# Layer 1's norm, half copies and value copies on ACT, early projections, late stores

## The chip, the core and the metric

The kernel runs on one core of a Trainium2 chip. The core has five engines with a queue of their own each: TensorE (PE, with its weight loads as PEld), VectorE (DVE), ScalarE (ACT), GpSimd (POOL) and SyncE (SP, which here issues DMAs). An engine works through its queue in order; a semaphore that it waits for holds up everything behind. The metric is the device time of the whole program in microseconds (us), less is better.

## The reference

The input is x, 32 x 256 x 128 in float32. Two transformer layers follow each other, each an attention part and a feed-forward part with a layer norm after each residual.

```python
# layer 0
qkv = x @ w_qkv + b_qkv          # 16 heads of 8; q and v also get a low-rank term
out = softmax(q k^T * 8**-0.5) v @ w_proj + b_proj
x = layernorm(x + out)
x = layernorm(x + experts(x))    # top-2 of 8 experts; one with over 1.25*tokens/8 tokens is dropped
# layer 1
q, k = rope(x @ w_q), rope(x @ w_k); v = x @ w_v      # causal, no bias
x = layernorm(x + softmax(masked q k^T * 8**-0.5) v @ w_proj)
x = layernorm(x + 0.1 * spline(x)) * gamma + beta
```

## The kernel before

Four stages run one after the other: attention of layer 0 (`attention`, "attn0"), the routing of the experts (`moe`), attention of layer 1 ("attn1") and the spline part with its norms. In `moe` only the routing is computed as a rule; a flag on the chip says whether any expert keeps its tokens, and here the branch with the experts isn't taken.

**An attention stage** is a pipeline over the 32 sequences. In a step st each engine works on several sequences at once, told apart by a lag: `st.has(2)` and `st.seq(2)` speak of the sequence that entered two steps ago. Lag 0: q and k, split in three bfloat16 parts by GpSimd, stored to `attn_scratch` in HBM and, at lag 1, loaded again by SyncE in six DMAs of 192 KB as stacks `q_st`, `k_st`. Lag 2: row scores (L665; in layer 1 with a mask, L661), whose maxima VectorE takes from three PSUM banks (L475), splits (L486, L488) and TensorE transposes (L594); ACT copies them (L451 for the first half of the heads, L426 for the second), SyncE places them in `q_st`. Values are projected (L631) and copied by VectorE (L499 in layer 0, L502 in layer 1). Lag 3: column scores (L687, mask L683), Exp on ACT (L419), value sums (L704). Lag 4: output copied (L441), transposed (L620), divided by VectorE (L509, L513), transposed (L638, copy L446), projected (L644), added to x (L528), statistics (L532, L538), norm.

The norm of layer 0 is GpSimd's (L338 to L367). In layer 1 GpSimd computes rstd (L338, L340) and VectorE the two tiles (L543, function `layer_norm`).

**The order in a step** is written by hand in the table `AT`: all engines count n from 0 to 15, one head's or unit's scores each, and an entry such as `act_mT1=1` says after which n the piece stands in that engine's queue. `pe_pv` does so for the value sums as (lag, unit). `pipeline` writes the first DEPTH steps out, then a loop of three steps, then the rest.

**Layer 1's q and k** are projected ahead for all sequences (`front`, TensorE L716). ACT copies those of sequences 0 to 2 straight to `qk` and, with the partition halves exchanged, to `q_half` (L388, L390); the others go to `probs` (L396) and in groups of four to HBM (`attn_qk_scratch`, L403, 1 MB each). Twenty are done before the first step, twelve within step 2, between its first row scores; in step 3 ACT waits for all stores before its first Exp. From sequence 3 on SyncE loads q and k (L237, 256 KB) and the two exchanged halves (L239, 128 KB each) one step ahead, and GpSimd rotates them: times sin (L311), times cos (L312), sum (L315). GpSimd then makes the parts (L320, L325, L329, L332), and in front of L325 it waits for the split of the first half's maxima, to leave VectorE alone.

## Time and profile before

| | us |
|---|---|
| median of 3 runs | 1414.62 |
| lowest, highest | 1412.3, 1417.19 |
| the profiled execution, its own time | 1410.58 |
| its span, first to last instruction | 1408.9 |
| busy in the span: PE, DVE, ACT, POOL | 1096.9, 1035.9, 778.3, 626.9 |
| mean granted TensorE clock | 0.885 |

Layer 0's attention lies at some 20 to 548 us of the span, the routing at 548 to 583, layer 1's attention at 583 to 1184, the spline part behind it. A busy time is the sum of an engine's instructions; idle time is told with what released the engine ("<-"). The granted clock is the share of 2.4 GHz that TensorE was given; 0.5 is 1.2 GHz.

### The profile page before, as it was taken

Reading aid. Unit: us, or ns where it says so; the run is one execution under the profiler, and the core shown is the slowest. Engines: PE = TensorE matmul, PEld = TensorE weight load, DVE = VectorE, ACT = ScalarE, POOL = GpSimd, SP = SyncE. Lnnn points to the kernel's source line nnn. Section 1 sums busy time; section 2 is a strip of 40 time slices with the busy share of each in tenths; the row PEclk is TensorE's granted clock in tenths of the full one; section 3 lists DMA queues with packets and bytes.
Section 4 is the critical chain, followed back from the end, with each engine's and each line's share of the span. In section 5 each row is a group of like instructions: output and inputs, shape, how many; then the busy total and the mean of one; then the engine's idle time right before and its main releaser. Section 6 shows DMA issues by size and latency. Waiting matters only on the chain. (4 is left out here: it accounts for less than half of the span.)

```text
span 1408.9 us, 36010 instructions
## 1 busy us (share of the span) xinstructions
PE 1096.9 (78%) x11349; PEld 803.1 (57%) x11349; DVE 1035.9 (74%) x2676; ACT 778.3 (55%) x1727; POOL 626.9 (44%) x845
## 2 busy tenths in 40 slices
PE   4799999999999996478888888888888897701330
PEld 3466666666666654356776777777777784401220
DVE  3688888888888871435877777777777772598886
ACT  2376776776776774335555555545555464500675
POOL 3245555555555532343544444444444414100666
PEclk9799999999999998798999999989999898855555
DMA  7545445445445410196656666655666521100012
GB/s 194 140 117 129 122 115 129 119 117 129 119 118 130 120 46 2 40 290 165 144 134 141 140 142 142 140 125 132 142 139 140 133 52 53 67 0 1 21 40 60
DMA packets 124967, 155.98 MB, mean 111 GB/s; under 512 B 13506, under 2 KB 100962, under 8 KB 115682
## 3 DMA queue, kind: packets, MB, share of 16 engines
q1 hardware_dynamic: 118114, 147.25, 42.8%
q10 hardware_dynamic: 6784, 7.86, 1.7%
q8 instruction: 36, 0.59, 0.2%
q14 instruction: 33, 0.27, 0.1%
HBM read 96.04 MB, written 45.35 MB: 100 GB/s over the span
## 5 line engine op out<-in xcount | busy, mean ns | idle before, releaser
L475 DVE TENSOR_REDUCE attn_negmax<-attn_row_ps 128x2 f32<-128x512 f32 (+1 forms) x1024 | 599.6, 618 | 202.5 <-PE attn_row_ps L665 190.6
L419 ACT ACTIVATE attn_probs<-attn_col_ps 128x512 f32<-128x512 f32 (+1 forms) x1024 | 532.9, 542 | 239.9 <-PE attn_col_ps L687 227.6
L687 PE MATMUL attn_col_ps<-q_st,k_st 74*128 74x256 bf16 (+1 forms) x2048 | 375.3, 265 | 16.4 <-ACT attn_probs L419 14.3
L665 PE MATMUL attn_row_ps<-k_st,q_st 72*128 72x256 bf16 (+1 forms) x2048 | 376.5, 266 | 8.8 <-DMA k_st<-attn_scratch 7.8
L687 PEld LDWEIGHTS attn_col_ps<-q_st,k_st 74*128 74x128 bf16 x2048 | 184.4, 100 | 99.5 <-ACT attn_probs L419 48.0
L704 PE MATMUL attn_out_ps<-attn_probs,v_sb 128*32 128x256 f32 (+1 forms) x4096 | 228.8, 356 | 0.7 <-ACT attn_probs L419 0.7
L665 PEld LDWEIGHTS attn_row_ps<-k_st,q_st 72*128 72x128 bf16 x2048 | 204.7, 100 | 36.6 <-issue 8.8
L661 PE MATMUL attn_row_ps<-mask_qk,ident_h 128*128 128x256 bf16 x512 | 147.3, 288 | 67.3 <-DVE attn_negmax L475 59.8
L704 PEld LDWEIGHTS attn_out_ps<-attn_probs,v_sb 128*32 128x32 f32 x4096 | 122.3, 110 | 71.1 <-issue 20.2
L325 POOL TENSOR_TENSOR attn_rest<-attn_qk,attn_parts 128x512 f32<-128x512 f32 x64 | 74.1, 1158 | 188.1 <-DVE attn_mparts L488 187.8
L683 PE MATMUL attn_col_ps<-mask_kq,ident_h 128*128 128x256 bf16 x512 | 147.3, 288 | 9.2 <-ACT attn_probs L419 5.1
L338 POOL TENSOR_SCALAR attn_var<-attn_mv 128x2 f32<-128x2 f32 x64 | 14.3, 223 | 292.8 <-DVE attn_mv L538 292.8
L543 DVE TENSOR_SCALAR x_mid<-attn_y_sb,attn_mv,attn_rstd 128x128 f32 (+1 forms) x64 | 70.7, 1145 | 39.8 <-POOL attn_rstd L340 39.8
L661 PEld LDWEIGHTS attn_row_ps<-mask_qk,ident_h 128*128 128x128 bf16 x512 | 51.5, 101 | 84.1 <-DVE attn_negmax L475 66.6
L1664 POOL TENSOR_TENSOR ffn_rstd<-ffn_var,minus_half 128x8 f32<-128x8 f32 x19 | 31.8, 1676 | 105.4 <-DVE ffn_var L1686 103.9
L332 POOL TENSOR_TENSOR attn_parts<-attn_rest,attn_parts 128x512 bf16<-128x512 f32 x64 | 74.0, 1156 | 5.4
L320 POOL TENSOR_SCALAR attn_parts<-attn_qk 128x512 bf16<-128x512 f32 x64 | 39.5, 617 | 68.2 <-ACT attn_qk L434 40.1
L683 PEld LDWEIGHTS attn_col_ps<-mask_kq,ident_h 128*128 128x128 bf16 x512 | 51.7, 101 | 27.7 <-issue 9.3
L1594 PE MATMUL ffn_o_ps<-ident_h,ffn_onehot 128*128 128x128 bf16 x64 | 10.1, 313 | 70.2 <-PEq L1345 70.2
L1605 PE MATMUL ffn_r_ps<-table_hm,ffn_ohT 128*128 128x193 bf16 x64 | 21.0, 361 | 55.9 <-ACT ffn_ohT L1617 55.9
L311 POOL TENSOR_TENSOR attn_q_half<-attn_q_half,sin 128x512 f32<-128x512 f32 x32 | 40.5, 1267 | 41.3 <-ACT attn_q_half L390 38.2
L446 ACT COPY attn_onT_sb<-attn_fin_ps 128x256 f32<-128x256 f32 x64 | 23.7, 370 | 60.0 <-PE attn_fin_ps L638 60.0
(232 smaller groups left out, 1668.8 us busy)
## 6 DMA issues: line engine op xcount, KB each, us to landing
q_st<-attn_scratch SPq DMA_DIRECT2D x192, 192.0 KB
k_st<-attn_scratch SPq DMA_DIRECT2D x192, 192.0 KB
attn_scratch<-attn_parts SPq DMA_DIRECT2D x64, 384.0 KB, 2.8
attn_scratch<-attn_parts SPq DMA_DIRECT2D x64, 128.0 KB, 2.8
attn_qk<-attn_qk_scratch SPq DMA_DIRECT2D x29, 256.0 KB, 7.6
attn_q_half<-attn_qk_scratch SPq DMA_DIRECT2D x58, 128.0 KB, 7.7
attn_qk_scratch<-attn_probs ACTq DMA_DIRECT2D x7, 1024.0 KB, 9.3
attn_xT<-x_mid SPq DMA_DIRECT2D x32, 128.0 KB, 2.4
```

What stands on the lines that cost most here:

```text
L311: nc.gpsimd.tensor_tensor(q_half_, q_half_, sin, ALU.mult).then_inc(sin_done, 1)
L320: nc.gpsimd.tensor_scalar(parts[:, :, 0, :], qk_, 1.0, 0.0, ALU.mult, ALU.add)\
L325: nc.gpsimd.tensor_tensor(rest[:, :, :], qk_, parts[:, :, 0, :], ALU.subtract)\
L332: nc.gpsimd.tensor_tensor(parts[:, :, 2, :], rest[:, :, :], parts[:, :, 1, :], ALU.subtract)\
L419: nc.scalar.activation(probs_of(st, 3, u)[:, j, 0:W], col_ps[:, n % 2, 0:W], ACT.Exp, scale=scale).then_inc(probs_kept, 1)
L475: nc.vector.tensor_reduce(negmax[:, t, 2 * p:2 * p + 2], row_ps[:, row_bank(st, u), 0:2 * keys].rearrange("p (a k) -> p a k", a=2), AX_X, ...
L543: nc.vector.tensor_scalar(x_all[:, bass.ds(st.seq(4, TB, t), 1), :].rearrange("p t c -> p (t c)"), y_sb[:, t, :], mv[:, t, 0:1], rstd[:, t ...
L661: nc.tensor.matmul(seen[:, :, keys - P:keys], ident_h[:, :], mask_qk[:, :, :], start=True, stop=False, skip_group_check=True)
L665: last = nc.tensor.matmul(bank[:, a * keys:(a + 1) * keys], q_st[0:KROWS, sl, h, t * P:(t + 1) * P], k_st[0:KROWS, sl, h, 0:keys], start=n ...
L683: nc.tensor.matmul(seen[:, :, 0:P], ident_h[:, :], mask_kq[:, :, :], start=True, stop=False, skip_group_check=True)
L687: last = nc.tensor.matmul(bank[:, t * N:(t + 1) * N - first], k_st[0:rows, sl, h, t * P:(t + 1) * P], q_st[0:rows, sl, h, first:N], start= ...
L704: last = nc.tensor.matmul(out_ps[32 * j:32 * j + 32, g * N + first:(g + 1) * N], v_sb[:, st.slot(lag), t, 32 * h:32 * h + 32], probs_of(st ...
```

## The change

- Layer 1's norm goes from VectorE to ACT (`ln_on="act"`): GpSimd also computes shift = -rstd * mean, and ACT writes rstd * y + shift. It runs one step later (`ln_lag=5`), so DEPTH is 6. Layer 0's stays on GpSimd at lag 4.
- Layer 1's value copies go from VectorE to ACT, after n=8.
- q_half is no longer loaded. ACT copies the halves from `qk` after n=15 (`HALF_ON="act"`), once its load has landed; GpSimd waits for these copies.
- 15 projections of layer 1 (0 to 14) move into `moe`, behind the last logits, and three groups are stored from there; the Exp of the second half of the routing (`weigh(1)`) stands after the fourth. 17 stand before layer 1's first step, none within step 2. The last four stores are issued in step 2, once the first stacks have landed, and each Exp group of step 3 waits for its own.
- `give` says at which GpSimd operations it waits for VectorE's split: in layer 0 before the third part (`lo`) instead of `rest`, in layer 1 before both.
- Several places in `AT` move by one to four.
- `probs`, `qk`, `q_half` are allocated once for both layers; the experts' buffers lie in `probs`. In the branch not taken here, the projections are done again.

```diff
-AT = {"attn0": dict(act_mT1=1, act_qk=(2, 4), act_oT=(4, 4), act_onT=8, act_mT0=11,
-                    dve_o=7, dve_split0=8, dve_split1=15, dve_v=5, dve_y=13, dve_var=15,
-                    pe_mT1=2, pe_qk=1, pe_oT=6, pe_v=5, pe_onT=8, pe_mT0=10, pe_y=12,
...
+AT = {"attn0": dict(act_mT1=2, act_qk=(3, 4), act_oT=(4, 5), act_onT=8, act_mT0=10, act_v=None, dve_o=6,
...
+                    pe_pv={8: [(3, 0), (3, 1)], 14: [(3, 2)], 4: [(4, 3)]}, give={"ln": [1], "lo": [0]}, ln_lag=4,
+                    ln_on="pool"),
...
+                    give={"lo": [0], "rest": [0]}, ln_lag=5, ln_on="act")}
+HALF_ON = "act"
-DEPTH = 5
+DEPTH = 6
-FRONT_EARLY = 20
+FRONT_MOE = 15
+STORED_MOE, STORED_LATE = 3, 4
...
-                for to, of_row in ((0, P // 2), (P // 2, 0)):
+                for to, of_row in ((0, P // 2), (P // 2, 0)) if HALF_ON == "dma" else ():
                     sp.dma_start(q_half[to:to + P // 2, sl, :, :].rearrange("p s n -> p (s n)"),
...
+                if ln_on == "act":
+                    pool.wait_ge(rstd_kept, st.seq(LN, c=1))
+                    nc.gpsimd.tensor_tensor(shift[:, :], rstd[:, :], mv[:, :, 0], ALU.mult).then_inc(product_kept, 1)
+                    pool.wait_ge(product_kept, st.seq(LN, c=1))
+                    apart(pool, mem)
+                    nc.gpsimd.tensor_scalar(shift[:, :], shift[:, :], -1.0, 0.0, ALU.mult, ALU.add)\
+                        .then_inc(shift_kept, 1)
...
+                        if HALF_ON == "dma":
+                            pool.wait_ge(qk_loaded[st.slot(0)], st.turn(0, 16 * QK_LOADS, -16 * QK_LOADS))
+                        else:
+                            pool.wait_ge(half_kept, st.seq(SLOTS, 2, 2))
...
+                    if fronted and not st.loop and st.off == 2 and n < PROBS:
+                        if n == 0:
+
+                            act.wait_ge(q_stacked[0], 16 * STACKS)
+                            act.wait_ge(k_stacked[0], 16 * STACKS)
+                        store_front(STORED_LATE + n)
...
+                    if fronted and HALF_ON == "act" and n == at["act_half"] and st.has(-1) and \
+                            (st.loop or st.off >= SLOTS - 1):
+                        sl = st.slot(-1)
+                        act.wait_ge(qk_loaded[sl], st.turn(-1, 16 * QK_LOADS, -16 * QK_LOADS))
+                        for to, of_row in ((0, P // 2), (P // 2, 0)):
+                            nc.scalar.copy(q_half[to:to + P // 2, sl, :, :].rearrange("p s n -> p (s n)"),
+                                           qk[of_row:of_row + P // 2, sl, :, :].rearrange("p s n -> p (s n)"))\
+                                .then_inc(half_kept, 1)
+                    if n == at["act_v"] and st.has(2):
+                        act.wait_ge(v_ready, st.seq(2, c=1))
...
+                    if ln_on == "act" and n == at["act_ln"] and st.has(LN):
+                        act.wait_ge(shift_kept, st.seq(LN, c=1))
...
+                pe.wait_ge(xT_kept, 2 * GROUPS)
+                for b in range(FRONT_MOE):
+                    if b >= 4:
+                        pe.wait_ge(front_kept, kept_by(b - 4))
+                    project(b, front_ready)
                 for half in range(2):
                     pe.wait_ge(routed, COUNTED * (half + 1))
...
-                weigh(1)
+                for b in range(FRONT_MOE):
+                    if b == WEIGH_BEFORE:
+                        weigh(1)
+                    act.wait_ge(front_ready, b + 1)
+                    keep_qk(b, front_kept)
```

Layer 1, ACT's queue from its second copy of the output (L441) to the end of a step; before, L451 and L446 are the copies of the maxima and of the transposed output.

```order
L441 COPY attn_oT_sb<-attn_out_ps 128x256
L419 ACTIVATE attn_probs<-attn_col_ps 128x384 x4
L451 COPY attn_mT_sb<-attn_in_ps 16x256
L419 ACTIVATE attn_probs<-attn_col_ps 128x384 x4
L446 COPY attn_onT_sb<-attn_fin_ps 128x256
L419 ACTIVATE attn_probs<-attn_col_ps 128x384 x2
```

The same stretch of the change, where L450 is the Exp, L504 and L477 the two copies named above.

```order
L472 COPY attn_oT_sb<-attn_out_ps 128x256
L450 ACTIVATE probs<-attn_col_ps 128x384 x4
L493 COPY v_sb<-attn_in_ps 128x8x2x8 x2
L498 ACTIVATE x_mid<-attn_y_sb,attn_shift,attn_rstd 128x128 x2
L450 ACTIVATE probs<-attn_col_ps 128x384
L504 COPY attn_mT_sb<-attn_in_ps 16x256
L450 ACTIVATE probs<-attn_col_ps 128x384 x4
L477 COPY attn_onT_sb<-attn_fin_ps 128x256
L450 ACTIVATE probs<-attn_col_ps 128x384 x2
L483 COPY q_half<-qk 64x512 x2
```

Four copies and two norm instructions have come in: values and norm behind the ninth Exp, the halves at the step's end.

The routing stage, TensorE's queue from the last logits to the counts, before:

```order
L883 MATMUL moe_t_ps<-ident,x_mid 128x128 x8
L895 MATMUL moe_g_ps<-x_all,moe_gate_T 32x256 x4
L905 MATMUL moe_l_ps<-ident,moe_gates_sb 128x128 x2
L905 MATMUL moe_l_ps<-ident,moe_gates_sb 128x128 x4
L912 MATMUL moe_g_ps<-moe_counts,moe_ones 128x8 x2
```

and in the change:

```order
L964 MATMUL moe_t_ps<-ident,x_mid 128x128 x8
L976 MATMUL moe_g_ps<-x_all,moe_gate_T 32x256 x4
L986 MATMUL moe_l_ps<-ident,moe_gates_sb 128x128 x2
L986 MATMUL moe_l_ps<-ident,moe_gates_sb 128x128 x4
L891 MATMUL moe_t_ps<-x_all,wqk 128x256 x30
L998 MATMUL moe_g_ps<-moe_counts,moe_ones 128x8 x2
```

Thirty projection matmuls, two a sequence, stand in front of the counts.

Layer 0, ACT's queue in the first third of a step: L426 copies the second half's maxima, L434 the projected q and k, L441 the output. Before:

```order
L419 ACTIVATE attn_probs<-attn_col_ps 128x512 x2
L426 COPY attn_mT_sb<-attn_fin_ps 16x256
L419 ACTIVATE attn_probs<-attn_col_ps 128x512
L434 ACTIVATE attn_qk<-attn_in_ps,bqk 128x256
L419 ACTIVATE attn_probs<-attn_col_ps 128x512 x2
L434 ACTIVATE attn_qk<-attn_in_ps,bqk 128x256
L441 COPY attn_oT_sb<-attn_out_ps 128x256 x2
```

In the change:

```order
L457 COPY attn_mT_sb<-attn_fin_ps 16x256
L450 ACTIVATE probs<-attn_col_ps 128x512
L465 ACTIVATE qk<-attn_in_ps,bqk 128x256
L450 ACTIVATE probs<-attn_col_ps 128x512
L465 ACTIVATE qk<-attn_in_ps,bqk 128x256
L472 COPY attn_oT_sb<-attn_out_ps 128x256
L450 ACTIVATE probs<-attn_col_ps 128x512
L472 COPY attn_oT_sb<-attn_out_ps 128x256
```

Three Exps stand before the copy of the maxima (L457) now instead of two, one Exp between it and the first of q and k as before, and an Exp has come between the two copies of the output.

## Rows read from the trace of the kernel before

**Rows 1.** Stretches: busy us (x count), PE, PEld, DVE, ACT, POOL; clock; DMA; GB/s.

```profile
100.00:493.00 393.00, 381.47 (x3896) 252.82 (x3895) 334.31 (x780) 280.36 (x598) 214.95 (x364) 1.00 0.50 122
614.00:632.50 18.50, 17.26 (x98) 13.35 (x99) 9.19 (x20) 6.75 (x12) 6.03 (x6) 0.90 0.89 268
699.80:1133.60 433.80, 377.16 (x4452) 311.26 (x4450) 335.46 (x800) 223.38 (x526) 205.11 (x225) 0.93 0.59 136
842.30:860.10 17.80, 15.58 (x178) 12.78 (x178) 13.36 (x33) 8.94 (x21) 8.20 (x9) 0.90 0.56 134
860.10:876.30 16.20, 13.93 (x178) 11.62 (x178) 13.30 (x34) 8.86 (x21) 8.22 (x10) 1.00 0.62 145
1136.70:1150.90 14.20, 13.86 (x180) 11.72 (x178) 11.29 (x33) 8.99 (x21) 0.93 (x2) 1.00 0.38 87
```

**Rows 2.** Groups of 699.8 to 1133.6 us, ACT: xcount, busy us, mean ns, idle before.

```profile
L446 ACT COPY attn_onT_sb<-attn_fin_ps 128x256 f32<-128x256 f32 x25 | 9.2, 367 | 0.0
```

**Rows 3.** Waits of 699.8 to 1133.6 us: us in total, times, longest.

```profile
PE attn_row_ps L661 <- DVE attn_negmax L475: 56.6, 25, 2.3
```

**Rows 4.** DVE and PE in time: start, us, engine, line; [idle before, releaser].

```profile
849.11 1.51 PE L704 MATMUL attn_out_ps<-attn_probs,v_sb 128*32 128x256 f32 x32
...
857.69 2.51 DVE L543 TENSOR_SCALAR x_mid<-attn_y_sb,attn_mv,attn_rstd 128x128 f32 x2 [1.25 <-POOL attn_rstd L340]
...
860.58 0.28 PE L661 MATMUL attn_row_ps<-mask_qk,ident_h 128*128 128x256 bf16 x1 [2.25 <-DVE attn_negmax L475]
...
1150.43 0.60 DVE L543 TENSOR_SCALAR x_mid<-attn_y_sb,attn_mv,attn_rstd 128x128 f32<-128x128 f32 x2 [1.25 <-POOL attn_rstd L340]
...
1151.42 0.28 PE L661 MATMUL attn_row_ps<-mask_qk,ident_h 128*128 128x256 bf16 x1 [0.35 <-DVE attn_negmax L475]
```

**Rows 5.** Line L543 (min/median/max ns), and GpSimd in order of time.

```profile
L543 DVE TENSOR_SCALAR x_mid<-attn_y_sb,attn_mv,attn_rstd x64: 341/1290/1308, 669.5 to 1182.7; 128x128 f32 x48, 128x128 f32<-128x128 f32 x16
...
857.62 1.27 POOL L311 TENSOR_TENSOR attn_q_half<-attn_q_half,sin 128x512 f32<-128x512 f32 x1
```

**Rows 6.** ACT at a step's end, in time; then lines L390 and L1624.

```profile
856.69 0.36 ACT L426 COPY attn_mT_sb<-attn_fin_ps 16x256 bf16<-16x256 bf16 x1 [0.57 <-PE attn_fin_ps L594]
...
L390 ACT COPY attn_q_half<-attn_col_ps x6: 577/580/582, 585.8 to 590.1; 64x512 f32<-64x512 f32 x6
...
L1624 ACT ACTIVATE ffn_z<-ffn_y,ffn_shift,ffn_rstd x64: 477/478/494, 1304.2 to 1394.3; 128x128 f32<-128x128 f32 x64
```

**Rows 7.** SyncE's issues in order of time; then landings of L237's loads.

```profile
857.08 0.70 SPq L249 DMA_DIRECT2D q_st<-attn_mT_sb  x1
...
860.60 0.38 SPq L237 DMA_DIRECT2D attn_qk<-attn_qk_scratch  x1
...
DMA to landing us min/median/max: 7.0/7.6/8.2
```

**Rows 8.** The change-over in order of time: ACT, TensorE, GpSimd, SyncE.

```profile
571.92 0.42 ACT L947 ACTIVATE moe_probs<-moe_left 128x256 f32<-128x256 f32 x1 [5.86 <-DVE moe_left L973]
...
583.15 3.75 PE L716 MATMUL attn_col_ps<-x_all,wqk 128*128 128x256 f32 x8 [2.74 <-PEq L1013]
...
587.11 1.27 POOL L311 TENSOR_TENSOR attn_q_half<-attn_q_half,sin 128x512 f32<-128x512 f32 x1 [38.23 <-ACT attn_q_half L390]
...
595.28 0.40 SPq L277 DMA_DIRECT2D attn_scratch<-attn_parts  x1
...
601.84 0.38 SPq L260 DMA_DIRECT2D q_st<-attn_scratch  x1
...
614.13 0.37 PE L661 MATMUL attn_row_ps<-mask_qk,ident_h 128*128 128x256 bf16 x1 [7.51 <-DMA k_st<-attn_scratch]
...
637.28 0.87 ACT L419 ACTIVATE attn_probs<-attn_col_ps 128x384 f32<-128x384 f32 x2 [6.99 <-DMA attn_qk_scratch<-attn_probs]
```

**Rows 9.** Waits of 100 to 480 us, TensorE's and ACT's.

```profile
PE attn_col_ps L687 <- ACT attn_probs L419: 10.4, 25, 0.5
...
ACT attn_mT_sb L426 <- PE attn_fin_ps L594: 29.0, 25, 1.2
```

More of the change, by code:

```diff
@@ L287, in step @@
             def step(st):
+                if LN == 5 and st.has(LN):
+                    finish_norm(st)
                 if st.has(4) and not fronted:
@@ L372, in _ @@
+                if LN == 4 and st.has(LN):
+                    finish_norm(st)
             pipeline(pool, step)
@@ L457, in _ @@
             if fronted:
-                for b in range(FRONT_EARLY):
+                for b in range(FRONT_MOE, B):
                     front(b)
@@ L562, in step @@
                         variance(st)
-                    if name not in LN_ON_POOL and n == at["dve_ln"] and st.has(4):
+                    if ln_on == "dve" and n == at["dve_ln"] and st.has(LN):
                         layer_norm(st)
@@ L721, in step @@
                 for n in range(H):
-                    if fronted and not st.loop and st.off == 2 and FRONT_EARLY + n < B:
-                        front(FRONT_EARLY + n)
                     if st.has(3):
@@ L754, in _ @@
             if fronted:
-                for b in range(FRONT_EARLY):
+                for b in range(FRONT_MOE, B):
                     front(b)
@@ L824, in moe, with front_bank, project, keep_qk @@
         e_h = sb("e_h", [P, MT, C])
-        e_hT = sb("e_hT", [P, MT * P])
-        e_y = sb("e_y", [P, MT, C])
-        e_acc = sb("e_acc", [P, MT, C])
         t_ps = ctx.enter_context(nc.psum_tensor("moe_t_ps", [P, 2, 2, 512], F32))
         g_ps = ctx.enter_context(nc.psum_tensor("moe_g_ps", [P, 2, 512], F32))
+        front_ready, front_kept, front_stored = (mem[k] for k in ("front_ready", "front_kept", "front_stored"))
+        redo_ready, redo_kept, redo_stored = sem("redo_ready"), sem("redo_kept"), [sem(f"redo_stored{n}") for n in range(STORED_MOE)]
+        qk, q_half, qk_dram = mem["qk"], mem["q_half"], mem["qk_dram"]
+        def front_bank(b):
+            return t_ps[:, b // 2 % 2, b % 2, :]
+        def project(b, ready):
+            for s in range(2):
+                last = nc.tensor.matmul(front_bank(b)[:, s * N:(s + 1) * N], mem["wqk1"][:, s, :], xT_all[:, b, :],
+                                        start=True, stop=True)
+            last.then_inc(ready, 1)
+        def keep_qk(b, kept):
+            of = front_bank(b)
+            if b < SLOTS:
+                nc.scalar.copy(qk[:, b, :, :].rearrange("p s n -> p (s n)"), of).then_inc(kept, 1)
+                for to, of_row in ((0, P // 2), (P // 2, 0)):
+                    nc.scalar.copy(q_half[to:to + P // 2, b, :, :].rearrange("p s n -> p (s n)"),
+                                   of[of_row:of_row + P // 2, :]).then_inc(kept, 1)
+            else:
+                nc.scalar.copy(stage[:, b - SLOTS, :], of).then_inc(kept, 1)
+        def store(act, n, stored):
+            first, to = STORED[n]
+            act.dma_start(qk_dram[first:to].rearrange("b p n -> p b n"), stage[:, first - SLOTS:to - SLOTS, :])\
+                .then_inc(stored, 16)
         l_ps = ctx.enter_context(nc.psum_tensor("moe_l_ps", [P, 2, 512], F32))
@@ L1128, in _ @@
                         nc.scalar.copy(xT_flat[:, n * 512:(n + 1) * 512], t_ps[:, 0, n % 2, :]).then_inc(again_kept, 1)
+                    for n in range(STORED_MOE):
+                        act.wait_ge(front_stored[n], 16)
+                    for b in range(FRONT_MOE):
+                        act.wait_ge(redo_ready, b + 1)
+                        keep_qk(b, redo_kept)
+                        n = group_ending(b)
+                        if n is not None:
+                            act.wait_ge(redo_kept, kept_by(b))
+                            store(act, n, redo_stored[n])
+                    for n in range(STORED_MOE):
+                        act.wait_ge(redo_stored[n], 16)
                 with act.Else():
```

209 lines of the change are left out of this document (119 added, 90 removed).

## The prediction

> **What bounds the kernel now.** I read the busy times by stretch first, then the waits of the long stretches, then the order of work in one step. In layer 0 TensorE is busy 381.5 of 393 us [rows 1] and its only wait of note is one of 0.4 us for ACT, once a step: 25 of them lie in 380 us [rows 9], so a step takes 15.2 us. In layer 1 no engine is full: TensorE 377 of 433.8 us, VectorE 335, ACT 223, GpSimd 205, and the granted clock is 0.93 [rows 1]. There 25 steps [rows 2] take 17.35 us each. The waits say why: in each of the 25 steps TensorE stands still 2.26 us (56.6 / 25) until VectorE frees a bank of row scores [rows 3]. The timeline shows what VectorE does meanwhile: it waits 1.25 us for the rstd from GpSimd, and its two norm instructions then take 2.51 us instead of the 0.60 us that they take at the end of the layer; there TensorE's stall is 0.35 us instead of 2.25 [rows 4].
>
> Two neighbouring steps show what the stall costs beyond itself. One takes 16.2 us at a granted clock of 1.00, the next 17.8 us at 0.90, with the same 178 matmuls [rows 1]: after some of the stalls TensorE runs at its lower level (1.2 GHz) for a while. A step of 14.2 us at 1.00, the one with the 0.35 us stall, exists at the layer's end [rows 1, 4]. So 17.35 is some 13.9 us of matmuls (TensorE's busy time at full clock), 2.3 us of stall and some 1.1 us of lower clock.
>
> **Layer 1, the norm.** It leaves VectorE: two instructions of 1.25 us, their wait of 1.25 us and, with them, two value copies. Why one takes 1.29 us as a rule and 0.34 at best: the median is the duration of the GpSimd multiplication that starts beside it (1.27 us) [rows 5]. VectorE waits for GpSimd here, and a norm on ACT ends that whatever ACT's price. The Trainium skill, page "SBUF — State Buffer", section "Who interferes with whom", says the same of the cause: such an instruction and a GpSimd one need one port pair, the later of the two blocks, and ACT is outside it. The page "ScalarE: Activation LUTs", section "Rules for kernel authors", speaks against the change: multiply, add and the like belong on VectorE. By it the norm should stay there, and by the rows without GpSimd beside it that would be cheaper (0.34 against 0.48 us); in this stretch the trace has 1.25 us, so the row decides.
>
> What it adds to ACT in a step: two norm instructions of 0.48 us, as the same operation takes in the last stage; two half copies of 64x512 that replace two DMAs, 0.58 us each from PSUM (from SBUF I allow 0.65); two value copies, each under the 0.36 us of a copy of 256 columns [rows 6]. That is 0.96 + 1.2 + 0.6 = 2.8 us on an engine that is busy 223 / 25 = 8.9 us a step, so 11.7 of 14.6: it doesn't bind by its sum, only by its place. GpSimd gets two small instructions more, at a place where it later waits for VectorE anyway; they cost nothing. VectorE keeps less than 335.5 - 50 x 1.25 = 273 us, 10.9 us a step.
>
> Place by place. Values and norm stand after the ninth Exp, and TensorE now has its value sums for two units there, 1.5 us [rows 4]. ACT's block is 1.5 us as well and TensorE may run two Exps ahead: hidden, but the transposed maxima behind it wait for the value copies; I allow 0.1 us. The half copies stand after the last Exp of a step. In front of TensorE there are the output projection and two heads of scores before it needs the next Exp, and ACT has some 0.6 us of slack there (its idle time before its next copy is of that size [rows 6]), so of the 1.2 us some 0.6 reach TensorE. The step becomes 13.9 + 0.6 + 0.1 = **14.6 us**, with no stall over 0.6 us; layer 0 has stalls of 0.4 us in each step and a clock of 1.00 [rows 1, 9], so I expect 1.00 here too. Ends: 14.0 (both hidden) and 16 (below). Gain: 25 x (17.35 - 14.6) = **68.8 us**.
>
> **The new wait.** ACT now waits for the load of q and k with its whole queue, the next step's Exps, behind it, and TensorE behind these. SyncE issues that load 3.5 us after the second half's maxima are handed over (857.08 to 860.60), and it lands 7.0 to 8.2 us later [rows 7]. From the hand-over to the landing: 3.5 + 7.6 = 11.1; then halves 1.2, Exp 0.5, scores and transposed maxima 1.2, their copy 0.4: a loop of 14.4 us, just under my 14.6. Two of nine DMAs, 256 of about 1,660 KB of a step's loads in that burst, are gone, which should take up to 1 us off the landing. So the loop doesn't bind, but has little room.
>
> **The change-over.** Removed: 20 projections before layer 1 and 12 between its first row scores. Now 15 run while VectorE routes, 17 follow, and half of their stores wait. The price first: four batches of copies (3 x 3 x 0.58 + 0.58 = 5.8 us, and 1 us until the first is there) stand before the Exp that VectorE's routing waits for, and ACT had only 5.9 us of idle time before it [rows 8]; the count matmul queues behind the last projection. I take +1.5 us; +7 if TensorE's clock stays low there. Then GpSimd starts its rotation at once, not 4.0 us into layer 1 (583.1 to 587.11). Its parts are stored from 595.28, the loads of the stacks start at 601.84, and the first row scores at 614.13 [rows 8]: 6.5 and 12.3 us beside stores of 1 MB. With at most two such stores around, I take 4 and 8.3: row scores at 583.1 + 1.5 + 8.0 + 0.3 + 4 + 8.3 = 605, 9 us earlier. The first step then has no projections in it (18.5 us before at 268 GB/s [rows 1]), but the late stores, 3.25 MB, start just then and share the queues with the next stack's 1.15 MB: 4.4 MB / 268 = 16 us for all, about 9 for the stacks if shared evenly, issued some 2 us in. Then half copies of 1.2 us. First Exp of the layer at 605 + 14 + 1 = 620 instead of 637.3, where ACT waited 7.0 us for the last store [rows 8]. Gain **17 us**; ends 8 (TensorE slow in the routing stage) and 24.
>
> **Layer 0.** ACT's copy of the maxima moves from behind the second Exp, where it waits 1.2 us a step for TensorE, to behind the third; with it goes the reason of TensorE's wait of 0.4 us [rows 9]. The other shifts by one place have slack of an Exp or more. The norm on GpSimd starts a little sooner; GpSimd's `rest` no longer gives way to VectorE, which may stretch a small cast. Of 30 x 0.4 = 12 I take **8 us**; ends 12 and -3. The end of layer 1 costs 0.5 us more (two GpSimd instructions and ACT's slower pair).
>
> **Sum.** 68.8 + 17 + 8 - 0.5 = 93.3 us off the profiled execution's 1410.6: 1317.3. The median of the runs is 4.0 us above that execution, so **1321 us**. Own range: steady step 14.2 to 15.1 (10 us down, 12 up), change-over 7 and 9, layer 0 4 and 11, hardly all on one side: 1303 to 1340.
>
> **Rivals.**
> A, 22%: the loop over the load binds. The landing is 8.6 us or more, since ACT's delay moves SyncE's bursts together, and steps take 15.4 to 16. At 15.7: 1321 + 25 x 1.1 = 1349. For it: 14.4 against 14.6. Against: fewer bytes, and landings within 7.0 to 8.2.
> B, 8%: ACT's bursts (2.8 us in two places) stall TensorE over 1 us, and its clock drops in every second step as now (1.6 us for 16.2 against 17.8). 13.9 + 1.2 + 0.8 + 0.1 = 16.0: 1321 + 35 = 1356. Against: the stalls of layer 0.
> C, 3%, slower: the same loop as in A, but with the load landing over 12 us after its issue. A step is then 6.8 + landing; the whole is slower than before once the step passes 17.35 + 24.5 / 25 = 18.3, a landing of 11.5. With 13 us: 19.8, so 25 x (19.8 - 14.6) = +130, 1451. For it: ACT waited 7.0 us for 1 MB stores. Against: no qk landing over 8.2 in 28.
> D, 2%: the change doesn't bring what it says: TensorE's stall only changes its releaser from VectorE to ACT at its old length; steps 17.3, and the change-over gains nothing either: within 4 us of 1415.
> The forecast has 65%.
>
> **How the numbers follow.** The likeliest case gives 1321. From 1303 up to 1352 takes in its range and most of A and part of B; some 1 in 6 is left out. About 0.3% (4 us) is what a measurement of this kernel can tell from no change: faster 0.95, same 0.02, slower 0.03.
>
> **What would show it.** Right: VectorE's releases of TensorE in layer 1 under 0.5 us a step, clock 1.00 there, steps of 14.4 to 14.8; ACT's idle time before the half copies near zero. A: ACT waits for the DMA of q and k in every step. B: clock 0.93 and TensorE waiting for ACT over 1 us. Change-over: first row scores near 605, first Exp near 620; wrong if the projections in the routing stage take 1.9 us each. Layer 0: TensorE's wait for ACT gone, steps of 14.8. Most open are the landing of the one load that ACT now waits for and the changed order in layer 0.

## The result, and the profile after

The changed kernel takes 1304.03 us (median of 4 runs, 1302.14 to 1305.4); the kernel before 1415.44 us beside it (4 runs, 1412.3 to 1417.19). The ratio is 0.9214, with a 95% interval of 0.9192 to 0.9236: 111 us less, where 94 were forecast. The profiled execution has a span of 1300.4 us against 1408.9, so 108.5 us to be explained.

Where they went, by marks that both traces have (the last reduction of layer 0 and the first Exp of each step of layer 1):

| stretch | before, us | after, us | difference | forecast |
|---|---|---|---|---|
| start to the last reduction of layer 0 | 521.8 | 497.5 | -24.3 | -8 |
| from there to layer 1's first Exp | 115.5 | 102.1 | -13.4 | -17 |
| its steps 1 to 4 | 62.5 | 60.5 | -2.0 | - |
| 25 steady steps of layer 1 | 433.8 | 365.6 | -68.2 | -68.8 |
| the rest | 275.3 | 274.7 | -0.6 | +0.5 |

The stretches of after in the columns of [rows 1] come first (span of the stretch; busy us and count of TensorE, its weight loads, VectorE, ACT and GpSimd; granted clock; DMA share; GB/s). The first is the start of layer 1, the second its 25 steady steps, the third 380 us of layer 0.

```profile
582.00:600.00 18.00, 9.02 (x61) 6.41 (x59) 8.69 (x20) 2.47 (x6) 4.30 (x5) 0.69 0.97 303
660.10:1025.70 365.60, 352.38 (x4445) 288.02 (x4445) 266.63 (x699) 281.88 (x674) 215.20 (x275) 1.00 0.59 144
100.00:480.00 380.00, 379.97 (x3992) 263.17 (x3992) 335.07 (x797) 278.01 (x612) 218.89 (x371) 1.00 0.53 130
```

A steady step of layer 1 takes 365.6 / 25 = 14.62 us at a granted clock of 1.00, where it took 17.35 at 0.93 [rows 1]. TensorE's wait in the same stretch, answering to [rows 3] (us in total, times, longest):

```profile
PE attn_col_ps L736 <- ACT probs L450: 12.5, 24, 1.5
```

The half copies (min/median/max ns) and what ACT waited for ahead of them (us, times):

```profile
L483 ACT COPY q_half<-qk x49: 616/616/617, 659.5 to 1011.2; 64x512 f32<-64x512 f32 x49
...
  DMA qk<-qk_scratch: 1.6, 2
```

TensorE waits no more for VectorE; what is left is 0.5 us a step for ACT. ACT waited for the load twice in 25 steps, 1.6 us together. The place of that last stall, in time (start, us, engine, line; in brackets the idle time before and its releaser):

```profile
864.70 1.26 ACT L483 COPY q_half<-qk 64x512 f32<-64x512 f32 x2
...
865.99 0.49 ACT L450 ACTIVATE probs<-attn_col_ps 128x384 f32<-128x384 f32 x1
866.53 0.10 PEld L736 LDWEIGHTS attn_col_ps<-mask_kq,ident_h 128*128 128x128 bf16 x1 [0.77 <-ACT probs L450]
866.53 0.28 PE L736 MATMUL attn_col_ps<-mask_kq,ident_h 128*128 128x256 bf16 x1 [0.49 <-ACT probs L450]
```

The half copies stand in front of the next step's first Exp, and TensorE waits for that Exp, as the sum had it (0.6 us there, 0.49 here). The change-over, answering to [rows 8]:

```profile
548.44 0.42 DVE L1069 TENSOR_REDUCE moe_total<-moe_probs 128x32 f32<-128x256 f32 x1 [1.21 <-ACT moe_probs L1033]
...
559.60 1.27 POOL L379 TENSOR_TENSOR q_half<-q_half,sin 128x512 f32<-128x512 f32 x1 [35.75 <-POOLq L1107]
...
567.77 0.40 SPq L289 DMA_DIRECT2D attn_scratch<-attn_parts  x1
...
571.72 0.38 SPq L272 DMA_DIRECT2D q_st<-attn_scratch  x1
...
581.50 3.60 ACTq L431 DMA_DIRECT2D qk_scratch<-probs  x4
581.57 0.37 PE L714 MATMUL attn_row_ps<-mask_qk,ident_h 128*128 128x256 bf16 x1 [4.71 <-DMA k_st<-attn_scratch]
...
590.36 0.75 SPq L280 DMA_DIRECT2D q_st<-attn_mT_sb  x1
...
597.91 1.26 ACT L483 COPY q_half<-qk 64x512 f32<-64x512 f32 x2 [8.94 <-DMA qk<-qk_scratch]
...
598.84 0.37 PE L736 MATMUL attn_col_ps<-mask_kq,ident_h 128*128 128x256 bf16 x1 [7.99 <-DMA q_st<-attn_mT_sb]
```

GpSimd starts its rotation with the layer, the stacks' loads start 4.0 us later than the store of the parts, and row scores start 9.85 us after that. Then TensorE waits 8 us for an 8 KB load (L280), issued beside 3.25 MB of late stores and right behind the next stacks' loads (1.15 MB), at 303 GB/s and a DMA share of 0.97.

Layer 0's surprise is in the waits of TensorE's weight loads. Those of 100 to 480 us, first of the kernel before, with its stretch:

```profile
PEld attn_col_ps L687 <- ACT attn_probs L419: 35.5, 76, 0.8
...
PEld attn_out_ps L704 <- ACT attn_probs L419: 5.3, 25, 0.2
```

```profile
100.00:480.00 380.00, 368.87 (x3760) 244.62 (x3759) 323.49 (x757) 271.24 (x577) 206.97 (x352) 1.00 0.50 123
```

and then of after:

```profile
PEld attn_col_ps L740 <- ACT probs L450: 21.9, 54, 0.4
...
PEld attn_out_ps L757 <- ACT probs L450: 0.2, 1, 0.2
```

Before, weight loads waited for ACT (35.5 + 5.3) / 25.1 steps = 1.63 us a step, while TensorE's own row showed 0.4 [rows 9]. After, it is 22.1 / 26.6 = 0.83, and TensorE has no idle row at all. Steps fell from 15.14 to 14.31 us. Half of the 0.83 us between the steps was hidden in busy time: 368.87 us / 3760 matmuls = 98.1 ns each before, 379.97 / 3992 = 95.2 ns after, at the same clock, which is 0.44 us over the 150 matmuls of a step.

### The profile page after: what moved, and what is told of

Its sections match the earlier page's. It is cut to its first block and busy times, and to the rows that moved or that the text cites. A ratio compares the mean times of both kernels' runs of the same rounds, so it can differ in the third digit from the quotient of the medians.

```text
span 1300.4 us, 36147 instructions
## 1 busy us (share of the span) xinstructions
PE 1060.4 (82%) x11349; PEld 785.9 (60%) x11349; DVE 948.1 (73%) x2548; ACT 841.0 (65%) x1913; POOL 640.9 (49%) x909
## 5 line engine op out<-in xcount | busy, mean ns | idle before, releaser
L450 ACT ACTIVATE probs<-attn_col_ps 128x512 f32<-128x512 f32 (+1 forms) x1024 | 531.0, 542 | 129.3 <-PE attn_col_ps L740 121.8
L718 PE MATMUL attn_row_ps<-k_st,q_st 72*128 72x256 bf16 (+1 forms) x2048 | 368.0, 261 | 8.3 <-DMA k_st<-attn_scratch 7.4
L740 PE MATMUL attn_col_ps<-q_st,k_st 74*128 74x256 bf16 (+1 forms) x2048 | 366.7, 260 | 3.2 <-ACT probs L450 1.5
L757 PE MATMUL attn_out_ps<-probs,v_sb 128*32 128x256 f32 (+1 forms) x4096 | 228.7, 356 | 0.7 <-ACT probs L450 0.7
L757 PEld LDWEIGHTS attn_out_ps<-probs,v_sb 128*32 128x32 f32 x4096 | 122.9, 109 | 66.8 <-issue 19.5
L736 PE MATMUL attn_col_ps<-mask_kq,ident_h 128*128 128x256 bf16 x512 | 141.7, 277 | 24.7 <-ACT probs L450 16.3
L307 POOL TENSOR_SCALAR attn_var<-attn_mv 128x2 f32<-128x2 f32 x64 | 14.4, 224 | 268.0 <-DVE attn_mv L591 268.0
L394 POOL TENSOR_TENSOR attn_rest<-qk,attn_parts 128x512 f32<-128x512 f32 x64 | 74.1, 1158 | 43.5 <-DVE attn_mparts L541 40.7
L390 POOL TENSOR_SCALAR attn_parts<-qk 128x512 bf16<-128x512 f32 x64 | 39.7, 621 | 60.3 <-ACT qk L465 43.2
L379 POOL TENSOR_TENSOR q_half<-q_half,sin 128x512 f32<-128x512 f32 x32 | 40.7, 1272 | 46.6 <-POOLq L1107 35.8
L477 ACT COPY attn_onT_sb<-attn_fin_ps 128x256 f32<-128x256 f32 x64 | 23.8, 372 | 59.7 <-PE attn_fin_ps L691 57.8
L472 ACT COPY attn_oT_sb<-attn_out_ps 128x256 f32<-128x256 f32 x128 | 47.1, 369 | 11.7 <-PE attn_out_ps L757 11.7
```

The costliest lines, as they stand in the source:

```text
L379: nc.gpsimd.tensor_tensor(q_half_, q_half_, sin, ALU.mult).then_inc(sin_done, 1)
L394: nc.gpsimd.tensor_tensor(rest[:, :, :], qk_, parts[:, :, 0, :], ALU.subtract)\
L450: nc.scalar.activation(probs_of(st, 3, u)[:, j, 0:W], col_ps[:, n % 2, 0:W], ACT.Exp, scale=scale).then_inc(probs_kept, 1)
L472: nc.scalar.copy(oT_sb[:, g * N:(g + 1) * N], out_ps[:, g * N:(g + 1) * N])\
L718: last = nc.tensor.matmul(bank[:, a * keys:(a + 1) * keys], q_st[0:KROWS, sl, h, t * P:(t + 1) * P], k_st[0:KROWS, sl, h, 0:keys], start=n ...
L736: nc.tensor.matmul(seen[:, :, 0:P], ident_h[:, :], mask_kq[:, :, :], start=True, stop=False, skip_group_check=True)
```

## The experiments

All start from one of the two kernels. Times are medians of 4 runs unless said otherwise, and a ratio is to the kernel before on the same chip. Step times are of the same marks as above. "After" is 1304.0 us, with steps of 14.31 us in layer 0 and 14.62 in layer 1.

### Is it the norm on VectorE, and is it GpSimd beside it?

The norm of layer 1 back on VectorE in the changed kernel:

```
-                    dve_split0=8, dve_split1=15, dve_v=None, dve_y=15, dve_var=15, dve_ln=None, pe_mT1=2, pe_oT=6,
+                    dve_split0=8, dve_split1=15, dve_v=None, dve_y=15, dve_var=15, dve_ln=15, pe_mT1=2, pe_oT=6,
...
-                    give={"lo": [0], "rest": [0]}, ln_lag=5, ln_on="act")}
+                    give={"lo": [0], "rest": [0]}, ln_lag=4, ln_on="dve")}
```

> The changed kernel with the norm of layer 1 back on VectorE, in the old place (behind the last reduction of the step, lag 4). Value and half copies stay on ACT. Theory (the norm on VectorE beside GpSimd's multiplication makes the stall): VectorE's two norm instructions take 1.25 us each again, TensorE waits some 2.2 us a step for VectorE, the clock falls to about 0.93 and steps take 17.0 to 17.5 us: 1304 + 25 x 2.6 = about 1370 us. Rival (the gain comes from value copies, halves and the new order of places): steps of at most 15.2, so 1304 to 1320 us.

And, in the kernel before, nothing but one more wait at the end of GpSimd's step, behind the rstd:

```
                     if name in LN_ON_POOL:
...
+                    else:
+                        pool.wait_ge(ln_kept, st.seq(4, TB, TB))
```

> The kernel before with one wait more: in layer 1 GpSimd starts no instruction of the next step until VectorE has finished its norm. Nothing else is moved. Theory (VectorE's norm is long only because a GpSimd instruction runs beside it): its two instructions take 0.6 to 0.7 us together instead of 2.5, TensorE's stall falls from 2.25 to about 0.4 us, the clock in layer 1 goes to 1.00 and steps from 17.35 to about 15 us: 1415 - 25 x 2.2 = about 1360 us. Rival (the wait of 1.25 us for the rstd and VectorE's own order make the stall): the stall stays above 1.5 us, and the time within 8 us of 1415; GpSimd's later start could cost up to 0.7 us a step on top, 1430.

Measured: 1371.1 us for the first (ratio to before 0.9662, interval 0.9634 to 0.9691), with steps of 17.06; 1359.9 us for the second (0.9595, 0.9568 to 0.9621), with steps of 15.14. Both fell on the theory's number. Of the first kernel, the norm on VectorE with its wait, the GpSimd instruction that starts beside it, and the stall behind it:

```profile
860.76 1.27 POOL L379 TENSOR_TENSOR q_half<-q_half,sin 128x512 f32<-128x512 f32 x1
860.83 2.52 DVE L596 TENSOR_SCALAR x_mid<-attn_y_sb,attn_mv,attn_rstd 128x128 f32 x2 [1.25 <-POOL attn_rstd L311]
...
863.73 0.28 PE L714 MATMUL attn_row_ps<-mask_qk,ident_h 128*128 128x256 bf16 x1 [1.61 <-DVE attn_negmax L528]
```

Over its 25 steps (columns as above) the clock is 0.96:

```profile
671.40:1098.00 426.60, 372.33 (x4445) 298.89 (x4445) 326.72 (x749) 264.54 (x624) 205.58 (x225) 0.96 0.51 123
```

Of the second, the same instruction (min/median/max ns), and then the two engines in time:

```profile
L545 DVE TENSOR_SCALAR x_mid<-attn_y_sb,attn_mv,attn_rstd x50: 337/345/348, 705.8 to 1070.6; 128x128 f32 x46, 128x128 f32<-128x128 f32 x4
```

```profile
871.12 0.61 DVE L545 TENSOR_SCALAR x_mid<-attn_y_sb,attn_mv,attn_rstd 128x128 f32 x2 [1.25 <-POOL attn_rstd L340]
...
871.89 1.27 POOL L311 TENSOR_TENSOR attn_q_half<-attn_q_half,sin 128x512 f32<-128x512 f32 x1 [0.80 <-DVE x_mid L545]
```

The wait of 1.25 us for the rstd is still there, and so is the norm on VectorE; only GpSimd is gone from beside it. The instruction takes 345 ns instead of 1290 [rows 5], and 2.2 us a step are saved by one wait. So the cause of the old stall is shown: the instruction beside it, not VectorE's work. The first run says the same from the other side: with all the rest of the change in place and the norm alone put back, a step is only 0.29 us shorter than before (17.06 against 17.35). This is what the Trainium skill, page "SBUF — State Buffer", section "Who interferes with whom", states of a `tensor_scalar` on VectorE beside GpSimd (the later one "fully blocks"); the trace agrees: the pair takes 2.52 us beside two GpSimd instructions of 1.27, and 0.61 with none. The second kernel's steps are 0.5 us longer than after's, and its waits name the reason:

```profile
PE attn_col_ps L685 <- DMA q_st<-attn_mT_sb: 24.5, 22, 1.9
```

1.0 us a step for the 8 KB load of the maxima, a wait that no row of before showed. The semaphore updates in the two traces say why: before, SyncE issued this load 8.2 us behind the load of q and k, and it landed in 2.0 us (medians of 25). Now it is issued 4.3 us behind and takes 4.6 us. The old stall had kept it clear of the loads ahead of it.

### What is ACT's norm worth, and what do the halves' loads cost?

The two put together: the changed kernel with the table of the first one (values and halves stay on ACT) and the wait of the second:

```
...
                 if LN == 4 and st.has(LN):
                     finish_norm(st)
+                    if ln_on == "dve":
+                        pool.wait_ge(ln_kept, st.seq(LN, TB, TB))
```

> The changed kernel with the norm of layer 1 on VectorE in its old place, and GpSimd held until that norm is done; values and halves stay on ACT. The run of the kernel before with this wait gave steps of 15.14 us, 1.0 us of which TensorE waited for the 8 KB load of the maxima, a wait that the halves' two loads brought. Theory (ACT's norm is worth no more than freedom from GpSimd's port; without the halves' loads the wait for the small load goes): steps of 14.6 to 14.9, 1304 to 1312 us. Rival (ACT's norm also saves VectorE's wait of 1.25 us for the rstd, which then holds TensorE up): steps of 15.3 or more, 1320 us or more.

And the changed kernel with the halves loaded:

```
-HALF_ON = "act"
+HALF_ON = "dma"
```

> The changed kernel with the exchanged halves of layer 1 loaded by two DMAs again instead of copied by ACT. If ACT's 1.2 us of half copies are TensorE's remaining stall of 0.5 us a step: stall gone, steps 14.1 to 14.2 instead of 14.6, 1304 - 25 x 0.45 = about 1293 us. Rival (TensorE then meets the next wait, GpSimd's chain behind three loads that land later): steps of 14.6 or more, 1304 to 1312 us.

The first gave 1306.8 us (ratio 0.9212, 0.9179 to 0.9244), steps of 14.70: the same as after, whose ratio is 0.9214. ACT's norm is therefore one of two ways to the same time. Its 25 steps (columns as above):

```profile
662.40:1029.90 367.50, 353.47 (x4445) 287.42 (x4445) 278.27 (x749) 262.90 (x623) 206.48 (x225) 1.00 0.59 143
```

ACT takes 502 ns for one tile; VectorE, undisturbed, takes 345. The row of after, then that of this run:

```profile
L498 ACT ACTIVATE x_mid<-attn_y_sb,attn_shift,attn_rstd x50: 487/502/516, 667.8 to 1019.8; 128x128 f32 x46, 128x128 f32<-128x128 f32 x4
...
L598 DVE TENSOR_SCALAR x_mid<-attn_y_sb,attn_mv,attn_rstd x50: 339/345/348, 664.7 to 1017.8; 128x128 f32 x48, 128x128 f32<-128x128 f32 x2
```

The Trainium skill, page "ScalarE: Activation LUTs", section "Rules for kernel authors", would keep this norm on VectorE. The runs here say that this costs nothing measurable once GpSimd is kept away, and 67 us if it isn't.

The second, with the halves loaded, was a miss for both theories: 1324.9 us (0.9362, 0.9309 to 0.9415), 21 us slower, steps of 15.26. ACT's 1.2 us were gone and TensorE's wait for ACT with them, but its waits read:

```profile
PE attn_col_ps L736 <- DMA q_st<-attn_mT_sb: 26.0, 22, 2.1
```

Its 25 steps with the rate of the DMA engines last, and its loads with KB each and the median from issue to landing:

```profile
666.80:1048.40 381.60, 354.31 (x4454) 289.59 (x4452) 268.38 (x697) 251.89 (x626) 214.98 (x275) 1.00 0.68 154
```

```profile
qk<-qk_scratch SPq DMA_DIRECT2D x24, 256.0 KB, 7.6
q_half<-qk_scratch SPq DMA_DIRECT2D x48, 128.0 KB, 7.8
```

Again 1.0 us a step for the 8 KB load, as in the kernel before with its wait. In after the same load held TensorE up once in 25 steps (0.2 us). It is issued 4.5 us behind the load of q and k in both kernels; by the semaphore updates it lands in 4.7 us with the halves' two loads (256 KB a step) between them and in 2.9 us without (medians of 25). That TensorE merely comes to it sooner is not the reason: in the run of the next section it comes sooner still, without these loads, and doesn't wait. I had expected the three loads to land late for GpSimd (7.8 us, against 7.3 of the one), and not that they delay the small one that TensorE needs. So taking them out is a gain of the change that my sum priced as a cost alone.

### A better place for the halves

If ACT's copies in front of the first Exp are the last stall, GpSimd can make them in the 4.0 us in which it waits for VectorE's statistics:

```
-HALF_ON = "act"
+HALF_ON = "pool"
...
             def step(st):
+                if fronted and HALF_ON == "pool" and st.has(0) and (st.loop or st.off >= SLOTS):
+                    sl = st.slot(0)
+                    pool.wait_ge(qk_loaded[sl], st.turn(0, 16 * QK_LOADS, -16 * QK_LOADS))
+                    pool.wait_ge(lo_kept, st.seq(1, c=1))
+                    for half, (to, of_row) in enumerate(((0, P // 2), (P // 2, 0))):
+                        if half:
+                            pool.wait_ge(half_kept, st.seq(SLOTS, 2, 1))
+                        apart(pool, mem)
+                        nc.gpsimd.tensor_scalar(q_half[to:to + P // 2, sl, :, :].rearrange("p s n -> p (s n)"),
+                                                qk[of_row:of_row + P // 2, sl, :, :].rearrange("p s n -> p (s n)"),
+                                                1.0, 0.0, ALU.mult, ALU.add).then_inc(half_kept, 1)
+                    pool.wait_ge(half_kept, st.seq(SLOTS, 2, 2))
+                    apart(pool, mem)
                 if LN == 5 and st.has(LN):
                     finish_norm(st)
```

> The changed kernel with the exchanged halves of layer 1 copied by GpSimd, at the start of its step, where it now waits 4.0 us for VectorE's statistics; ACT copies none. Theory (ACT's 1.26 us of halves in front of the next step's Exps make TensorE's last stall of 0.5 us a step; GpSimd's idle time takes 2 x 0.6 us without harm): TensorE's wait for ACT gone, steps of 14.0 to 14.2 instead of 14.6, 1304 - 25 x 0.5 = about 1292 us. Rival (GpSimd's copies run beside VectorE's last instructions of the step and hold them up, or start only when the load has landed and push the norm and the rotation back): steps of 14.6 or more, 1304 to 1320 us.

Measured: 1287.7 us (5 runs, 1285.25 to 1290.65; ratio 0.9083, 0.9055 to 0.9111), the fastest of all, 16 us below after. Steps are 14.03 us. The stretch of its 25 steps comes first, then GpSimd and VectorE in time:

```profile
660.60:1011.40 350.80, 349.52 (x4452) 288.38 (x4450) 268.27 (x701) 252.24 (x625) 245.69 (x325) 1.00 0.62 150
```

```profile
856.92 0.62 POOL L358 TENSOR_SCALAR q_half<-qk 64x512 f32<-64x512 f32 x1 [1.59 <-DMA qk<-qk_scratch]
857.08 0.69 DVE L541 TENSOR_REDUCE attn_negmax<-attn_row_ps 128x2 f32<-128x512 f32 x1 [0.19 <-PE attn_row_ps L731]
857.68 0.41 DVE L594 TENSOR_TENSOR attn_y_sb<-attn_fin_ps,x_mid 128x256 f32<-128x256 f32 x1
857.73 0.61 POOL L358 TENSOR_SCALAR q_half<-qk 64x512 f32<-64x512 f32 x1 [0.19 <-POOL q_half L358]
...
859.30 0.22 POOL L307 TENSOR_SCALAR attn_var<-attn_mv 128x2 f32<-128x2 f32 x1 [0.95 <-DVE attn_mv L604]
```

TensorE is busy 349.5 of 350.8 us; layer 1 is now bound by it as layer 0 is. It never stands still for the 8 KB load, which lands in 2.9 us as in after. GpSimd's copies run beside a reduction and an addition of VectorE whose durations are what they are elsewhere (0.69 and 0.41 us), and GpSimd still waits 0.95 us for the statistics. The rival had no effect here.

### Where do layer 0's 24 us come from?

Its whole table back to the places of before (with GpSimd's giving way), the places that differ drawn together in two lines:

```
-  act_mT1=2, act_qk=(3, 4), act_oT=(4, 5), act_mT0=10, dve_o=6, dve_v=7, dve_y=12, dve_var=13,
-  pe_qk=0, pe_oT=7, pe_v=6, give={"ln": [1], "lo": [0]}
+  act_mT1=1, act_qk=(2, 4), act_oT=(4, 4), act_mT0=11, dve_o=7, dve_v=5, dve_y=13, dve_var=15,
+  pe_qk=1, pe_oT=6, pe_v=5, give={"rest": [0], "ln": [1]}
```

> The changed kernel with layer 0's places and GpSimd's giving way as before (all else as changed). Theory (layer 0's 24 us come from its table alone): steps of 15.1 us instead of 14.3 in layer 0, 1304 + 30 x 0.8 = 1328 us. Rival (they come from elsewhere, such as the buffers or the pipeline that is one step deeper): steps stay at 14.3, 1304 us.

Then parts of it. ACT's three places of the first third of a step alone (`act_mT1`, `act_qk`, `act_oT` of the lines with + above):

> The changed kernel with three of layer 0's places on ACT as before: the copy of the second half's maxima behind the second Exp instead of the third, the first biased copy of q and k and the two copies of the value sums one place earlier. Theory (ACT waits there for TensorE, and the Exps behind it then hold TensorE up three times a step, most of it as waits of the weight loads): steps of 15.0 to 15.2 in layer 0 instead of 14.3, 1304 + 30 x 0.8 = 1328 us, and weight loads waiting for ACT 1.6 us a step instead of 0.8. Rival (VectorE's places or GpSimd's giving way made the gain): steps of 14.3 to 14.4, 1304 to 1308 us.

VectorE's four with `pe_oT` and `pe_v`:

> The changed kernel with VectorE's places of layer 0 (reciprocal and product of the sums, values, residual, variance) and the two places of TensorE that go with them as before. Theory (ACT's places alone make layer 0's gain): steps of 14.3 to 14.4, 1304 to 1308 us. Rival (they come from these places): steps of 14.9 or more, 1320 us or more.

`give` alone:

> The changed kernel with GpSimd giving way in layer 0 before its third instruction on the parts (the rest) again instead of before the last one. Theory (GpSimd has idle time in every step): steps of 14.3, 1304 us within 4. Rival (the earlier landing of the parts lets TensorE go on): over 1310 us.

| layer 0 | time, us | ratio, 95% interval | step, us | weight loads' wait for ACT, us a step |
|---|---|---|---|---|
| after | 1304.0 | 0.9192 to 0.9236 | 14.31 | 0.83 |
| whole table back | 1333.5 | 0.938 to 0.9427 | 15.16 | 1.78 |
| ACT's three places back | 1327.9 | 0.9319 to 0.9406 | 14.93 | 1.54 |
| VectorE's places back | 1314.6 | 0.9229 to 0.9293 | 14.47 | 0.87 |
| `give` back | 1305.2 | 0.9169 to 0.9247 | 14.31 | 0.83 |

The table alone makes layer 0's gain. ACT's three places make 0.62 of 0.85 us a step, VectorE's with TensorE's two 0.16 (where the forecast had put nothing), and GpSimd's giving way nothing; `act_mT0` and `pe_qk` were not moved by themselves. The median of the run with VectorE's places back lies between its two cases, 10.6 us above after, and only 5 of these are 30 x 0.16. In its trace the layer's first step, from the first sequence's first Exp to the second's, takes 19.6 us against 13.8 in after. That step took 14.4 us in the kernel before and 19.3 in the same kernel with the wait on GpSimd in layer 1, whose layer 0 is the same, so it varies without any change of places. It also makes 3.6 of the 29.5 us of the whole table. The row of the third line, against that of after above:

```profile
PEld attn_col_ps L740 <- ACT probs L450: 39.2, 77, 0.8
```

And the other way round, in the kernel before: the wait on GpSimd as above, and ACT's three places (the other entries of the line left out).

```
-  act_mT1=1, act_qk=(2, 4), act_oT=(4, 4)
+  act_mT1=2, act_qk=(3, 4), act_oT=(4, 5)
```

> The kernel before with two edits: GpSimd held in layer 1 until VectorE's norm is done (as in the run with that wait alone, 1360 us), and ACT's three places of layer 0 as in the changed kernel (copy of the maxima behind the third Exp, the first biased copy and the copies of the value sums one place later). Theory (ACT's places act by themselves): layer 0's steps fall from 15.14 to 14.5 us, 1360 - 30 x 0.64 = about 1340 us. Rival (they only help together with TensorE's and VectorE's new places): steps of 15.0 or more, 1355 to 1362 us.

Measured: 1345.5 us (0.9466, 0.9418 to 0.9515), 14.4 us below the kernel with the wait alone (18 by the ratios; the two ran on different chips); steps of 14.67 in layer 0. It lies between the two cases: by themselves ACT's places bring 0.47 us a step, not 0.62, so the rest of the table seems to help them. TensorE has hardly any idle time in its stretch (0.75 of 380 us), yet its steps are 0.36 us longer than after's, which stands in busy time again (379.25 / 3882 = 97.7 ns a matmul):

```profile
100.00:480.00 380.00, 379.25 (x3882) 252.91 (x3879) 330.62 (x778) 278.60 (x596) 214.26 (x364) 1.00 0.51 127
```

Weight loads wait for ACT 0.94 us a step there and 0.83 in after. So that wait tells of ACT's places, not of the whole difference between two kernels.

### The change-over

No store held back: with `STORED_LATE` at 8 each group is stored once it is copied.

```
-STORED_MOE, STORED_LATE = 3, 4
+STORED_MOE, STORED_LATE = 3, 8
...
-                        if n == 0:
-
-                            act.wait_ge(q_stacked[0], 16 * STACKS)
-                            act.wait_ge(k_stacked[0], 16 * STACKS)
-                        store_front(STORED_LATE + n)
+                        act.wait_ge(front_kept, kept_by(B - 1))
...
-                                act.wait_ge(front_stored[STORED_LATE + u], 16)
+                                act.wait_ge(front_stored[4 + u], 16)
```

> The changed kernel with no store held back: each group of projections is stored as soon as it is copied. Theory (the DMA engines are busy 0.97 in this stretch, so the order of the same bytes moves little in the sum): the stacks' loads land 4 to 8 us later, first row scores at about 588 instead of 582, but the 8 KB load then meets no stores; first Exp within 3 us of 599.6, time 1302 to 1307 us. Rival (holding back is what brings the change-over's gain): first Exp at 606 or later, 1310 us or more.

And the four late stores divided, the last two behind the place of `act_mT0`:

```
-                        store_front(STORED_LATE + n)
+                        if n < 2:
+                            store_front(STORED_LATE + n)
...
+                    if fronted and not st.loop and st.off == 2 and n == H - 1:
+                        act.wait_ge(m_placed[0][st.slot(2)], 16)
+                        for late in range(STORED_LATE + 2, len(STORED)):
+                            store_front(late)
```

> The changed kernel with the four late stores of layer 1's projections divided: two at once as now, the other two (1.25 MB) only when the first 8 KB load of the maxima has landed. Theory (the change-over's late part is the 8 KB load waiting 8.5 us behind 3.25 MB of stores): it lands 3 to 5 us earlier, and the first Exp of the layer comes 3 us earlier; the Exps of the third unit then wait up to 2 us for their store: 1301 us, within 3. Rival (the DMA engines are full there whatever the order): 1304 to 1308 us.

At once: 1306.5 us (0.9181 to 0.9243). From layer 0's last reduction, row scores start at 86.5 us instead of 84.1, the first Exp at 103.5 instead of 102.1 and the steady steps at 166.8 instead of 162.6. Divided: 1304.4 us (0.9175 to 0.9238), row scores at 83.9, first Exp at 100.7, given back in the next step (18.8 us instead of 16.8). Neither time can be told from after. That the load would land 3 to 5 us earlier was wrong. In the divided kernel the 8 KB load is issued at 589.83 and TensorE still waits for it:

```profile
589.83 0.75 SPq L280 DMA_DIRECT2D q_st<-attn_mT_sb  x1
...
597.65 0.37 PE L741 MATMUL attn_col_ps<-mask_kq,ident_h 128*128 128x256 bf16 x1 [6.27 <-DMA q_st<-attn_mT_sb]
```

With 1.25 MB less beside it, it is there 7.8 us after its issue instead of 8.5. Nor are the late stores what makes it late. With all stores issued at once the last of them has landed at 591.3, and the load still takes as long:

```profile
591.56 0.31 SPq L272 DMA_DIRECT2D q_st<-attn_scratch  x1
...
594.43 0.75 SPq L280 DMA_DIRECT2D q_st<-attn_mT_sb  x1
...
602.07 0.37 PE L732 MATMUL attn_col_ps<-mask_kq,ident_h 128*128 128x256 bf16 x1 [6.83 <-DMA q_st<-attn_mT_sb]
```

What the three kernels have in common is the load of q and k, behind the next stacks' 1.15 MB, issued under 1 us ahead of it; in a steady step it is issued 4.5 us ahead, and the 8 KB land in 2.9. Holding stores back brings 1.4 us at the first Exp and 4.1 at the steady steps in these traces, where the medians differ by 2.5 us. What is left of the change-over's 13.4 us is put down to the earlier projections by subtraction, since no run moved them alone. Part of it seems to hang on layer 0's places: in the trace with ACT's three back the first Exp comes at 106.4, in that with the whole table back at 105.2. Nor were the value copies on ACT or layer 1's other places in `AT` tried by themselves.

## Why the prediction was right, and where it missed

The forecast was 1321 us with a range of 1303 to 1352; 1304 lies at its lower end. Of the 17 us between 1321 and 1304 layer 0 makes 16, and the change-over takes back 4. The first steps of layer 1 make 2, the tail 1, and 2 are the gap between the profiled execution and the median, 1.9 us here where 4.0 had been taken. So one term lay far outside its own end, and that the time still falls inside the range is in part luck.

**Layer 1's norm and the steady step: right in mechanism and size.** 14.62 us against 14.6, a granted clock of 1.00, 68.2 us against 68.8. The parts are 14.1 us of busy time and 0.5 of stall, where the sum had 13.9, 0.6 and 0.1: two small errors that cancel. The two runs on the norm show the cause, and the run with the halves on GpSimd shows the stall of 0.5 us that the sum charged to them. One part of the picture was incomplete: the halves' two loads were counted only for the landing of q and k, and would have cost 1.0 us a step through the 8 KB load once VectorE's stall was gone. The remedy that the text looked at, ACT, was also not the only one; a wait on GpSimd gives the same.

**The new wait on the load (rivals A and C): did not come.** The loop was put at 14.4 us against a step of 14.6. ACT waited for the load twice, 1.6 us in 25 steps, and the landing was 7.3 us where 7.6 had been used (9.1 at the longest, beyond the 8.6 of rival A, but not as a rule). **Rival B** (bursts of ACT over 1 us, clock down): stalls were 0.5 us on average and 1.5 at the longest, and the clock stayed up. **Rival D** is excluded by the time.

**Layer 0: the term that was mis-sized.** "Of 30 x 0.4 = 12 I take 8 us", with an end of 12; it brought 24.3. The step that failed is the reading of [rows 9]: TensorE's own wait of 0.4 us was taken for all that ACT's copies cost. The weight loads waited 1.63 us a step for the same Exps, in four places (76 and 25 waits in 25 steps), and only one of these showed as idle time of TensorE; the others spread the matmuls out inside its busy time. "The other shifts by one place have slack" was wrong as well for VectorE's, which with TensorE's two are worth 0.16 us a step. That the waits of weight loads are what stretches the busy time is read from their going together: both rise when ACT's places alone go back (1.54 us, steps 0.62 longer). That layer 0 was "busy 381.5 of 393 us" [rows 1] seemed to leave no more than 12 us; it left 24.

**The change-over: 13.4 us instead of 17.** The routing stage lost little (59.1 us from the last reduction to the flag before, 59.3 after; 1.5 had been taken). Row scores came 8.2 us earlier against the sum's 9: the parts took 4.0 us as assumed, the stacks 9.85 instead of 8.3. From there to the first Exp it was 18.0 us, not 15: the bytes were counted (16 us for 4.4 MB), but not that an 8 KB load issued close behind the stacks' loads takes 8 us.

**The tail** was 0.6 us shorter where 0.5 longer was expected.

## What to carry to other kernels

A busy engine can still lose time: where TensorE's idle rows are small, read what its weight loads wait for, and compare busy time per matmul at the same clock between stretches. Where a VectorE instruction has two durations, look for the GpSimd instruction beside it before moving work; one wait that keeps them apart may give what a new home for the work gives. When a stall is taken away, ask which transfers will now be issued closer together, small ones behind large ones above all.
